# Output rows of a fusion block: ten SyncE stores against 34 GpSimd indirect transfers of 128 rows

## The reference, cut to what matters

```python
def _L0_ffn_ref(x, Wg, bg, W1, b1, W2, b2):
    ...
    for e in range(E):
        h = jax.nn.gelu(xf @ W1[e] + b1[e], approximate=False)
        out = out + w_dense[:, e:e + 1] * (h @ W2[e] + b2[e])
    return out.reshape(B, L, D)
...
    h = h + _L0_ffn_ref(_layernorm(h, axis=-1), ...)
    return h
```

## Time and profile before

| What | Value |
|---|---|
| time, median of 3 runs | 264.91 us (263.81 to 265.07) |
| the profiled execution's own time | 263.95 us |
| its span | 262.2 us |
| granted TensorE clock, mean | 0.976 of full speed |
| busy: PE, DVE, ACT, POOL | 240.2, 180.9, 155.2, 98.1 us |
| DMA traffic | 14.41 MB, mean 55 GB/s |

### The profile page before, as it was taken

One profiled execution on the slowest core, in us unless ns is written; L12 is line 12 of the kernel. 1 busy time (PEld: TensorE's weight loads), 2 busy tenths in 40 slices (PEclk: granted clock), 3 DMA queues, 4 the chain that ended last, 5 costly groups with the idle time before them and its releaser, 6 DMA issues.

```text
span 262.2 us, 4569 instructions
## 1 busy us (share of the span) xinstructions
PE 240.2 (92%) x1523; PEld 127.5 (49%) x1523; DVE 180.9 (69%) x558; ACT 155.2 (59%) x285; POOL 98.1 (37%) x87
## 2 busy tenths in 40 slices
PE   7678988889589799989999999999999999999993
PEld 5466776466345575454464433443334333434551
DVE  2798897999997998999788298955318613622223
ACT  2976775895637795376447454464654745465660
POOL 2200056336843530537813115865225232153332
PEclk9999997999959999999999999999999999999998
DMA  7740000000000000530000750014901039200502
GB/s 219 210 175 5 0 2 0 2 0 0 4 0 0 4 0 4 157 87 2 0 1 8 186 135 0 2 30 108 217 3 38 4 94 229 45 0 5 160 0 63
DMA packets 12358, 14.41 MB, mean 55 GB/s; under 512 B 6096, under 2 KB 9984, under 8 KB 12208
## 3 DMA queue, kind: packets, MB, share of 16 engines
q1 hardware_dynamic: 11760, 13.66, 20.3%
q10 hardware_dynamic: 576, 0.47, 0.7%
HBM read 12.87 MB, written 1.25 MB: 54 GB/s over the span
## 4 chain that ended last, share of the span: by engine, by line
PE 62%; DVE 24%; issue 6%; ACT 3%; POOL 2%; DMA 2%; POOLq 0%; DVEq 0%
PE ps L996 24%; PE ps L1009 22%; DVE arena L538 3%; DVE stat L557 2%; PE ps L929 2%; DVE trig L671 2%; DVE early L661 2%; DMA phase<-in_phase 2%; ACT early_p L422 2%; PE ps L963 1%; PE ps L918 1%; PE ps L955 1%; PE ps L858 1%; POOL rstd L356 1%; DVE xn L576 1%
## 5 line engine op out<-in xcount | busy, mean ns | idle before, releaser
L504 ACT ACTIVATE arena<-ps,cols 128x1024 f32<-128x1024 f32 (+2 forms) x80 | 74.6, 982 | 50.6 <-PE ps L996 30.6
L996 PE MATMUL ps<-xt,w 64*128 64x512 f32 (+2 forms) x320 | 70.0, 554 | 0.2
L386 POOL TENSOR_TENSOR acc<-acc,vs 128x512 f32<-128x512 f32 (+2 forms) x35 | 39.0, 1113 | 71.8 <-DVE vs L759 71.2
L1009 PE MATMUL ps<-arena,w 128*64 128x512 f32 (+2 forms) x320 | 65.0, 538 | 0.0
L759 DVE SCALAR_TENSOR_TENSOR vs<-ps,b_col,wide 128x512 f32<-128x512 f32 (+2 forms) x35 | 23.2, 666 | 34.6 <-PE ps L1009 33.6
L996 PEld LDWEIGHTS ps<-xt,w 64*128 64x128 f32 x320 | 27.5, 185 | 32.1 <-issue 22.9
L356 POOL TENSOR_TENSOR rstd<-vare,minus_half 128x8 f32<-128x8 f32 (+2 forms) x15 | 26.2, 1746 | 44.4 <-DVE vare L566 44.4
L1009 PEld LDWEIGHTS ps<-arena,w 128*64 128x64 f32 x320 | 20.2, 136 | 38.6 <-issue 35.2
L374 POOL TENSOR_TENSOR early<-early,turn_n 128x544 f32<-128x544 f32 x8 | 11.6, 1452 | 30.9 <-DVE early L665 30.9
L422 ACT ACTIVATE early_p<-ps,negmax 72x144 f32<-72x144 f32 x32 | 11.6, 372 | 3.6 <-DVE negmax L602 3.4
L759 DVE SCALAR_TENSOR_TENSOR acc<-ps,b_col,wide 128x512 f32<-128x512 f32 (+2 forms) x5 | 3.4, 670 | 13.7 <-DMA wide<-rows_of 10.2
(11 more groups left out here) (138 smaller groups left out, 392.9 us busy)
## 6 DMA issues: line engine op xcount, KB each, us to landing
wide<-rows_of SPq DMA_DIRECT2D x24, 256.0 KB, 5.9
wide<-rows_of SPq DMA_DIRECT2D x8, 192.0 KB, 4.4
w<-in_w SPq DMA_DIRECT2D x1, 1024.0 KB, 5.3
wide<-rows_of SPq DMA_DIRECT2D x8, 128.0 KB, 3.1
out<-res SPq DMA_DIRECT2D x6, 128.0 KB, 2.1
h0s<-in_txt SPq DMA_DIRECT2D x1, 512.0 KB, 7.2
w<-in_w SPq DMA_DIRECT2D x1, 512.0 KB, 6.1
arena<-in_x_a SPq DMA_DIRECT2D x1, 288.0 KB, 4.4
```

The costliest lines, as they stand in the source:

```text
L386: pool.tensor_tensor(acc[:, g % 2, 0:128 * GW[g]], acc[:, g % 2, 0:128 * GW[g]], scaled[:, i % 2, 0:128 * GW[g]], ALU.add).then_inc(S["acc ...
L504: act.activation(hidden_e[:, k % 4, 0:2 * n].rearrange("p (h t) -> p h t", h=2), ps[:, 2 * j:2 * j + 2, 0:n], ACT.Gelu, bias=col("b1", 2 * ...
L996: ins = pe.matmul(ps[:, 2 * j + h, 0:n], w1[r, c:c + 128], xt[r, GC[g]:GC[g] + n], start=True, stop=True)
L1009: ins = pe.matmul(ps[64 * h:64 * h + 64, OUT_BANK[i % 2], 0:n], w2[:, 2 * (i % E) + j, :], hidden_e[:, (2 * i + j) % 4, n * h:n * h + n], ...
```

## The change

SP's stores are taken out. POOL gets a part in stage `finish`: it waits for `out_sb`, and then starts, for every window of the group and each half, one indirect transfer of 128 rows, whose target rows are read from a column of the new table `row_id`. That table (128 partitions by 34 numbers) is made by one `iota` ahead of POOL's other work; entry (p, 17h + w) is 2176h + 128w + p. SP waits at the end for 34 transfers instead of ten.

```diff
@@ -207,6 +207,7 @@
         wsp = sb("wsp", [128, 4, 16])
+        row_id = sb("row_id", [128, 2 * NWIN], mybir.dt.uint32)
         wt = sb("wt", [16, 2, 512])
@@ -322,12 +323,7 @@
             for g in range(NG):
                 if g + 1 < NG:
                     spread_weights(g + 1)
-                sp.wait_ge(S["out_sb"], g + 1)
-                for h in range(2):
-                    dst = out[COLS * h + GC[g]:COLS * h + GC[g] + 128 * GW[g], :]
-                    src = res[:, cut(g)].rearrange("p (w h d) -> p w h d", h=2, d=64)[:, :, h, :]
-                    sp.dma_start(dst.rearrange("(w p) d -> p w d", p=128), src).then_inc(S["stored"], 16)
-            sp.wait_ge(S["stored"], 16 * 2 * NG)
+            sp.wait_ge(S["stored"], 16 * 2 * NWIN)
@@ -345,6 +341,9 @@
             pool.memset(gate_w[:, :, :], 0.0).then_inc(S["zeros"], 1)
+
+            link(pool.iota(row_id[:, :].rearrange("p (h w) -> p h w", h=2), [[COLS, 2], [128, NWIN]], base=0,
+                           channel_multiplier=1))
 
             pool.wait_ge(S["base_trig"], 1)
@@ -385,6 +384,14 @@
                                        scaled[:, i % 2, 0:128 * GW[g]], ALU.add).then_inc(S["acc_sb"], 1)
+                elif stage == "finish":
+                    pool.wait_ge(S["out_sb"], i + 1)
+                    for w in range(GC[i] // 128, GC[i] // 128 + GW[i]):
+                        for h in range(2):
+                            k = NWIN * h + w
+                            pool.indirect_dma_start(out[:, :], bass.IndirectOffsetOnAxis(ap=row_id[:, k:k + 1], axis=0),
+                                                    res[:, 128 * w + 64 * h:128 * w + 64 * h + 64], None)\
+                                .then_inc(S["stored"], 16)
```

## The result

| | before | after |
|---|---|---|
| time, median of 4 runs | 264.99 us | 281.33 us (280.98 to 283.23) |
| ratio | | 1.0635 [1.0572, 1.0698] |
| the profiled execution, its span | 263.95, 262.2 us | 281.12, 279.2 us |
| start of `finish:3` on PE, to the span's end | 256.68, 5.5 us | 259.52, 19.7 us |

What follows compares the result with a forecast made beforehand. PE's matmuls bound the kernel until about 256 us, then a bare tail of stores. Tail 12.4 plus middle 0.7 gave 13.1 us, so 278.0 us on the median; range 270 to 291 us, forecast's chance 0.62.

Steps and rivals of the forecast that it cites:

- The 12 transfers in a row with nothing beside them: After POOL's last addition, `finish:3`'s 8 and `finish:4`'s 4 transfers run in a row from about 258 us.
- the addition of step 13 at 179: Sign at `finish:0`: POOL's addition of step 13, queued behind six transfers, stands at about 179 us.
- one short PE wait near 187: Sign at `finish:0`: a first PE wait near 187 us, under 1 us, for the bank of step 18.
- The tail, forecast +12.4: Behind POOL's last addition at 258.1 us: 12 transfers replace four SP stores, 12c - 2.0, so +12.4 us at c = 1.2.
- 2.1 us for landing and end: At the span's end: time kept behind the last issue, from SP's last store, 2.6 us less 0.5 for issue.
- c = 1.2 us: Price of one indirect transfer on POOL: 1.12 us as for 4 powers in each partition, plus 0.1 us hand-over.
- cheap issue: Rival: a transfer costs 0.48 us like SP's issue; +3.8 us in the tail, nothing in the middle, 268.7 us; chance 0.15.
- dear issue: Rival: each transfer holds POOL 2.1 us; +23.2 us in the tail, +34.2 in sum, 299.1 us; chance 0.20.
- `finish:0`, forecast 0.7: Middle, group 0: six transfers delay POOL's additions and root, so PE waits 0.7 us in all.
- Contention: DVE and POOL hold each other up when both read two operands; nothing added, left to the range.
- `finish:1` and `finish:2`, forecast free: Middle, groups 1 and 2: eight transfers each, hidden under PE's matmuls, no cost; `finish:2` free up to c = 1.5.
- The matmuls' end: Sign: the forecast is wrong if PE's matmuls end later than about 257 us.

Runs made afterwards that it cites:

- experiment 7: The changed kernel with its 34 transfers as plain ones on POOL, without the index: 271.39 us, ratio 1.0201 to the kernel before.
- experiments 2 and 8: First: changed kernel, SP storing groups 0 to 2, 12 indirect transfers left, 279.56 us. Second: kernel before, its ten large stores issued by POOL, 266.72 us.
- experiment 1: The changed kernel run once more with no edit, as control: 280.93 us, ratio 1.0609 to the kernel before.
- the middle alone: Third experiment: changed kernel with POOL's indirect transfers for groups 0 to 2 only (22 of 34), SP storing groups 3 and 4: 266.56 us, ratio 1.0071.
- 5 and 12: Kernel before, both: first, POOL zero-fills where transfers of groups 0 to 2 would stand, 265.84 us; second, `finish:3` earlier, one last store on ACT, 264.36 us.

## Why the prediction was right, and where it was off

**Right: the place, the form and the range.** The 12 transfers in a row with nothing beside them, the tail about four times as long, the addition of step 13 at 179, one short PE wait near 187, and the rest of the middle within a microsecond or so. Sum 13.1 us forecast; 16.0 to 16.3 measured. The profile's 17.0 are 3.9 us over the sum: 1.8 in the tail, 1.4 in the middle and 0.7 of the start's scatter.

**The tail, forecast +12.4, measured +14.2 in the profile; alone, +14.6 by the medians and +13.2 in its profile.** Three things make the 1.8 us of the profile. The spacing is 1.265 us, not 1.2: 11 x 0.065 = 0.7. POOL's first start comes 0.28 us after the data, not 0.04. And the end: I kept 2.1 us for landing and end behind an issue of 1.2, 3.3 us after the last start, and it is 279.2 - 275.12 = 4.1 us. I had taken that term from SP's stores, where no drain stood behind the landing; behind 34 transfers of POOL one does, in after and in the plain transfers of experiment 7. With 12 or 10 of them (experiments 2 and 8) it ends 0.4 us after SP's release and costs nothing, so it goes with their number; why, the runs don't say.

**The price, right in size and wrong in kind.** c = 1.2 us was taken from POOL's row of four powers, because an address for each partition looked like work for each item. A transfer with half the rows costs 0.07 us less, not half. What costs is a fixed part, and more than half of it (0.73 of 1.265 us) appears only in the indirect form. That POOL makes addresses from the table stays a supposition; what is shown is that hardly any of its time goes by the row. Had I taken SP's issue as POOL's plain price, I would have been close (0.48 and 0.53) and then had no row for the rest; it was luck that the wrong analogue gave the right number. The rival *cheap issue* is refuted by the same spacing; so is *dear issue*: landing took 2.2 us from the last start to SP's release (277.3 - 275.12), and the transfers overlap in it. In the profile of experiment 1, which has the landings, they took 2.1 us. The Trainium skill (DMA: Bandwidth & Descriptors, "Anatomy of one DMA") has a fixed cost of about 2.0 us for such a transfer; the trace agrees with that as the time to land, and shows that it isn't paid in a row: twelve took 14.9 us (261.19 to 276.08), not 24. Of the profile's record the Trainium skill (Perfetto Trace Analysis, "DMA Instruction — SWDGE (GPSIMD)") says that it ends when the descriptors are written, not when the data has moved; 0.96 us of record against 2.2 us to the release agrees.

**`finish:0`, forecast 0.7.** Measured 0.65 and 0.6 in two profiles of the changed kernel, 1.7 in the middle alone. A small term that I left out lies in it: "Contention ... I add nothing". Two operations of DVE's statistics, on 8 numbers for each partition, took 0.60 us beside POOL's second residual addition and 1.12 us beside that of step 15 (183.53 above), where both took 0.17 before. That 0.65 came out so near to 0.7 is in part luck. In the two profiles of the changed kernel POOL's block begins 5.8 us behind the start of PE's transposes, where the forecast had 6.6. In the middle alone it is 6.9, and there the stage costs 1.7 us: 0.4 more than forecast by the spacing, 0.3 by the later start, and the rest is of the size of this term.

**`finish:1` and `finish:2`, forecast free.** Right at this price: the middle alone has 24.83 and 32.81 us between its marks, as before. The 0.56 and 0.93 us of the first profile are not in the second, but for 0.7 in the third part, with the wait for `wide`. In the first, ACT and DVE began work late there without a cause that the profile names: 214.5 and 238.9 us. For higher prices the prediction left `finish:1` out. PE's step 25 needs its bank there when it starts in the timeline of before:

```profile
215.93 1.94 PE L1009 MATMUL ps<-arena,w 128*64 128x512 f32 x8
```

By the prediction's own working DVE's step 23 ends at 201.4 + 8c + 2.05, so the stage is free only up to c = 1.56, and costs 1.9 us at 1.8 and 4.3 at 2.1. The range's upper end should have been 293 us and *dear issue* 303; the forecast at c = 1.2 is not touched.

**The matmuls' end.** The prediction called itself wrong if they ended later than 257. They ended at 259.6, 2.8 us later than before. 0.7 is the start's scatter, the 2.1 is told above. So the sign did point at something: the middle was forecast 1.4 us too low for this profile, and 0.6 and 1.0 us too low for those of experiments 1 and 3. The sign was set too tightly: a mark at a fixed time also carries all that varies before it; the difference of two marks would have been the right sign.

**What stays open.** Whether POOL's held time is the whole of the middle's 1.6 us; what holds POOL for the 0.73 us that the indirect form adds; why the closing drain is late behind 34 of POOL's transfers and not behind 12; and what holds ACT, DVE and PE, for 4 us and more, around the end of blocks of eight indirect transfers.

## What to carry to other kernels

A store that nothing follows is paid in full, so count what is issued behind the last computation, and multiply by the issuing engine's time per transfer: the number of transfers, the engine and the form (plain or indirect) decide, and much less the size (0.53 us for 128 rows, 0.73 for 256 to 512, on POOL). A transfer through an index is for rows whose places aren't known; where they are, a plain store of many windows does with two issues of 0.5 us on an idle queue what cost POOL 1.27 us six to eight times. If POOL must start them, put them singly behind its other work, not as a block ahead of an addition that others wait for, and leave as few as possible for the end.

## What the runs showed of the hardware that I had not expected

- POOL's time for an indirect transfer hardly depends on its rows: 0.866, 0.892 and 0.962 us for 32, 64 and 128, and 0.30 us idle between two of them. Plain ones took 0.53 us with no gap. The first of a kernel took 1.20 us (indirect) or 0.75 us (plain), the first of a later block hardly more than the others (0.98 to 1.04 us, indirect).
- After 34 transfers of POOL the program ends later than the landing: from SP's release to the closing step it was 1.8 us (277.3 to 279.1) and with 34 plain ones 1.8 us as well (266.4 to 268.2), against 0.7 us with SP's ten stores. With 12 indirect or ten plain ones on POOL it was 0.6 us.
- Around the end of blocks of eight indirect transfers ACT stood idle without a cause in the program, and PE waited for it: up to 3.9 us at 32 rows, 1.7 us at 64, and at 128 rows under 1 us in one profile and not at all in the others. It was not seen with plain transfers or spread ones. The fewer rows, the worse, in one profile of each: cutting three quarters of the written bytes made the kernel some 7 us slower. Waits of PE for ACT of 0.3 us come without such transfers too (5 and 12).
- A DVE operation on 8 numbers for each partition took 1.12 us instead of 0.17 beside a POOL addition that reads two operands, and another 0.60.
